# A two-layer recurrent kernel: four chunks' gated products halved by GpSimd for f16 down products, gates turned sooner

## The reference

```python
xn = layernorm(x)
# recurrent part
x_in, res = split(xn @ W_in)                    # 256 channels each
xc = silu(causal_conv4(x_in) + conv_b)
p = xc @ W_x                                    # low rank 16, B 16, C 256
delta = softplus(p[:16] @ W_dt + b_dt)
h = h * delta_t + B_t * x_t                     # per step of the sequence
y = h.sum(states) * C_t
s = (y * silu(res)) @ W_out
# experts: 2 shared and 16 routed, 64 wide
shared = gelu(xn @ shared_up) @ shared_down
gate = top 4 of softmax(xn @ router_w.T), others 0
routed = sum over experts of (gelu(xn @ up) * gate) @ down
x = x + s * silu(shared + routed)
```

## Time and profile before

| what | value |
|---|---|
| median of 3 runs | 686.22 us (683.71 to 689.05) |
| the profiled execution, whole | 683.87 us |
| its span, first to last instruction | 682.1 us |
| TensorE matmul busy | 630.9 us, 93% |
| VectorE busy | 630.7 us, 92% |
| ScalarE busy | 506.7 us, 74% |
| GpSimd busy | 280.0 us, 41% |
| granted TensorE clock, mean | 0.999 of full |
| start of the second layer's body 1 | 291.79 us |

### The profile page before, as it was taken

How to read it: one execution, slowest core, us unless ns; L and a number is a source line. 1 busy time by engine, 2 the same in 40 slices (tenths; PEclk the granted TensorE clock), 3 DMA queues, 4 the chain that set the end, 5 groups by cost and what they waited for, 6 DMA issues and landing times. The chain is left out here.

```text
span 682.1 us, 10868 instructions
## 1 busy us (share of the span) xinstructions
PE 630.9 (93%) x2714; PEld 301.5 (44%) x2714; DVE 630.7 (92%) x1470; ACT 506.7 (74%) x808; POOL 280.0 (41%) x275
## 2 busy tenths in 40 slices
PE   4779999999999997889999999999999999999985
PEld 2334444444444443444444444444444444444442
DVE  4999999999999999989999999999999999999866
ACT  2846666666666665887887888888789788888874
POOL 6557777777676765133122212303303221230220
PEclk9999999999999999999999999999999999999999
DMA  7331000000000000000000000000000000000000
GB/s 174 106 94 31 0 1 0 0 0 0 0 0 0 0 0 0 1 1 0 17 17 0 16 15 0 16 15 0 15 15 15 0 15 15 0 15 15 0 16 31
DMA packets 10739, 11.29 MB, mean 17 GB/s; under 512 B 4800, under 2 KB 6288, under 8 KB 10720
## 3 DMA queue, kind: packets, MB, share of 16 engines
q1 hardware_dynamic: 9744, 10.73, 5.3%
q0 software_dynamic: 112, 0.33, 0.1%
q10 hardware_dynamic: 864, 0.00, 0.1%
HBM read 6.87 MB, written 4.19 MB: 16 GB/s over the span
## 5 line engine op out<-in xcount | busy, mean ns | idle before, releaser
L1177 PE MATMUL bank<-arena,w 128*128 128x512 f16 x640 | 148.6, 379 | 4.0 <-DVE arena L788 4.0
L1177 PE MATMUL bank<-arena,dnT 128*128 128x512 f32 x288 | 138.6, 592 | 0.0
L662 ACT ACTIVATE arena<-bank,xinv 128x512 f32<-128x512 f32 x144 | 94.8, 688 | 37.7 <-PE bank L1177 37.5
L444 POOL TENSOR_TENSOR arena<-arena 128x512 f32<-128x512 f32 x48 | 59.7, 1273 | 135.5 <-ACT arena L599 135.5
L1177 PEld LDWEIGHTS bank<-arena,w 128*128 128x128 f16 x640 | 62.5, 98 | 78.2 <-issue 10.0
L491 ACT ACTIVATE arena<-bank 128x512 f16<-128x512 f32 x96 | 53.9, 607 | 35.6 <-PE bank L1177 35.6
L434 POOL TENSOR_TENSOR arena<-arena 128x512 f32<-128x512 f32 x16 | 16.8, 1051 | 151.6 <-DVE arena L1025 151.6
L1177 PEld LDWEIGHTS bank<-arena,dnT 128*128 128x128 f32 x288 | 53.7, 191 | 35.9 <-issue 21.2
L1177 PE MATMUL bank<-arena,wsqT 128*128 128x512 f32 x128 | 64.5, 608 | 4.7 <-DVE arena L797 4.7
L1034 DVE SCALAR_TENSOR_TENSOR arena<-bank,cws,arena 128x506 f32<-128x506 f32 (+1 forms) x96 | 67.0, 740 | 1.1
L788 DVE SCALAR_TENSOR_TENSOR arena<-bank,arena 128x512 f16<-128x512 f32 x96 | 60.2, 670 | 2.4 <-ACT arena L491 1.2
(11 more groups left out here) (223 smaller groups left out, 1497.7 us busy)
## 6 DMA issues: line engine op xcount, KB each, us to landing
x_all<-in_L_attn_x SPq DMA_DIRECT2D x16, 256.0 KB, 2.6
out<-x_all SPq DMA_DIRECT2D x16, 256.0 KB, 2.0
up_n<-in_L_ffn_routed_up SPq DMA_DIRECT2D x1, 512.0 KB, 4.0
dn_n<-in_L_ffn_routed_down SPq DMA_DIRECT2D x1, 512.0 KB, 5.6
wx<-in_L_attn_W_x SPq DMA_DIRECT2D x1, 288.0 KB, 2.8
k_u<-in_L_ffn_k POOLq DMA_DIRECT2D x1, 256.0 KB, 5.7
w_in<-in_L_attn_W_in SPq DMA_DIRECT2D x1, 256.0 KB, 2.7
k_u<-in_L_ffn_k SPq DMA_DIRECT2D x1, 128.0 KB, 6.6
```

The source lines that it names most:

```text
L444: g.tensor_tensor(prod[:, c, :], act[:, c + 1, :], gate[:, :], ALU.mult).then_inc(sem["b_actp"], 1)
L662: a.activation(act[:, c, :], q_U[(c + 1) % 2][:, :], ACT.Gelu, scale=xinv[:, I_UP:I_UP + 1]).then_inc(sem["b_act"], 1)
L1177: return nc.tensor.matmul(ps, lhsT, rhs, start=start, stop=stop)
```

## The change

GpSimd now has four chunks (GP = 4, chunks 1 to 4) and splits each product into two f16 halves: a product in f32 into `pp` (two buffers), a copy to f16 (`ph`) and the rest as f16 (`pl`). It does this in two pairs per body: chunks 3 and 4 of group m behind the square root for the next group's normalisation, and chunks 1 and 2 of group f behind the spreading of f's gates. VectorE keeps chunks 5 to 8. Down products 1 to 4 become three f16 matmuls each, with weights `dnH` and `dnL`; 0 and 5 to 8 stay f32. To keep halves in range, the down weights are scaled by a power of two, the gates by another, and `ffn_silu` undoes both through its scale; the largest down weight is found by one more Abs pass on ScalarE. The gates are turned behind up product 3 and copied behind Gelu 4 (before: 5 and 8). The up products use three banks in turn, `q_D[0]` and both `q_U`, except in body 0, and down products 5 and 6 move between 2, 3 and 4. The diff, cut to its core:

```diff
@@ build
-    GP = 3
+    GP = 4
     GV = RC - GP
@@ tiles
-        prod = tile(1, [P, RC, N])
+        prod = tile(1, [P, GV, N])
+        pp = tile(1, [P, 2, N])
+        ph = tile(1, [P, GP, N], F16)
+        pl = tile(1, [P, GP, N], F16)
@@ banks
+        q_E = (q_D[0], q_U[0], q_U[1])
+        def up_bank(n, c):
+            return q_U[(c + 1) % 2] if isinstance(n, int) and n == 0 else q_E[c % 3]
@@ GpSimd
+            def gated_halves(m, c):
+                def product(c):
+                    pool.wait_ge(sem["b_act"], UC * m + c + 2)
+                    if not c % 2:
+                        after(pool, sem["b_down"], UC * m if c else UC * (m - 1) + 3)
+                    pool.wait_ge(sem["b_gate"], m + 1)
+                    if c % 2:
+                        pool.wait_ge(sem["b_p"], GP * m + c)
+                    g.tensor_tensor(pp[:, c % 2, :], act[:, c + 1, :], gate[:, :], ALU.mult).then_inc(sem["b_p"], 1)
+                def high(c):
+                    g.tensor_scalar(ph[:, c, :], pp[:, c % 2, :], 1.0, None, ALU.mult).then_inc(sem["b_ph"], 1)
+                def low(c):
...
+                    g.tensor_tensor(pl[:, c, :], pp[:, c % 2, :], ph[:, c, :], ALU.subtract).then_inc(sem["b_actp"], 1)
+                product(c)
+                product(c + 1)
+                high(c)
+                low(c)
+                high(c + 1)
+                low(c + 1)
             def layer1(n):
-                if has(m):
-                    for c in range(GP):
...
-                        g.tensor_tensor(prod[:, c, :], act[:, c + 1, :], gate[:, :], ALU.mult).then_inc(sem["b_actp"], 1)
                 if has(f) and has(f + 1):
                     spread_of_rows(f + 1, "b_")
+                if has(m):
+                    gated_halves(m, 2)
                 if has(f):
                     spread_gates(f)
+                    gated_halves(f, 0)
@@ ScalarE
-                    a.activation(gate[:, :], q_Q[:, :], ACT.Copy).then_inc(sem["b_gate"], 1)
+                    a.activation(gate[:, :], q_Q[:, :], ACT.Copy, scale=down[:, GATE_S:GATE_S + 1]).then_inc(sem["b_gate"], 1)
-                    a.activation(gp[:, :], q_F[:, :], ACT.Silu).then_inc(sem["b_g"], 1)
+                    a.activation(gp[:, :], q_F[:, :], ACT.Silu, scale=down[:, SUM_S:SUM_S + 1]).then_inc(sem["b_g"], 1)
                         if c == 5 and has(f + 1):
                             turned_high(f + 1, 1 - par, q_D[1])
-                    gates_out()
+                        if c == 4:
+                            gates_out()
@@ VectorE
             def down_out(i):
-                v.tensor_copy(dnT[:, i * WB * P:(i + 1) * WB * P], q_W[UB + i][:, 0:WB * P]).then_inc(sem["prep_out"], 1)
+                for c in full:
+                    at_c = max(0, c - GP) * P
+                    last = v.tensor_scalar(dnT[:, at_c:at_c + P], q_W[UB + i][:, c * P - at:(c + 1) * P - at],
+                                           col(down, SHARED_S) if c == 0 else col(wsc, I_DN), None, ALU.mult)
+                if split:
+                    w = slice((split[0] - 1) * P, split[-1] * P)
+                    last = halves(dnH[:, w], dnL[:, w], q_W[UB + i][:, w.start + P - at:w.stop + P - at], col(wsc, I_DN))
+                last.then_inc(sem["prep_out"], 1)
                     gated(GP + 3)
-                    gated(GP + 4)
@@ TensorE
-            DOWN_BEHIND = {1: 5, 3: 6, 6: 7, 7: 8}
+            DOWN_BEHIND = {0: 4, 5: 7, 7: 8}
                 def low_rank():
                     after(pe, sem["b_cr"], IC * m)
+                    if not (isinstance(m, int) and m == 0):
+                        pe.wait_ge(sem["b_act"], UC * m + UC - 2)
                 def expert_in(c):
...
+                    elif c >= 3:
+                        pe.wait_ge(sem["b_act"], UC * f + c - 2)
+                    elif c:
+                        pe.wait_ge(sem["b_conv"], IC * f * (TAPS - 1) + CONV_DONE[c - 1])
                     else:
+                        pe.wait_ge(sem["b_cr"], IC * m + IC)
                 def expert_out(c):
...
+                    if 0 < c <= GP:
+                        mm(q_F[:, :], dnH[:, w], ph[:, c - 1, :], False, False)
+                        mm(q_F[:, :], dnH[:, w], pl[:, c - 1, :], False, False)
+                        last = mm(q_F[:, :], dnL[:, w], ph[:, c - 1, :], False, False)
                     expert_out(2)
+                    expert_out(5)
                     expert_out(3)
-                    expert_out(4)
+                    expert_out(6)
-                    if has(f) and c == 5:
+                    if has(f) and c == 3:
                         gates_turned()
```

More of the change, by code:

```diff
@@ L59, in build @@
     assert G % 2 == 0
-    GP = 3
+    GP = 4
     GV = RC - GP
-    I_IN, I_UP, I_RW, I_WX, I_DT, I_CW, I_CB = range(7)
-    NSC = 7
+    I_IN, I_UP, I_RW, I_WX, I_DT, I_CW, I_CB, I_DN = range(8)
+    NSC = 8
     XC_S, C_FAC, B_FAC, D_FAC = range(4)
+    SHARED_S, SUM_S, GATE_S = range(3)
     x_d = A["L0_attn_x"].rearrange("b t c -> (b t) c").rearrange("(g p j) c -> g p (j c)", p=P, j=J)
@@ L133, in build @@
         fac = sb("fac", [P, 4])
+        down = sb("down", [P, 3])
         cws = sb("cws", [P, IC, TAPS])
-        dnT = sb("dnT", [P, UC * P])
+        dnT = sb("dnT", [P, (UC - GP) * P])
+        dnH = sb("dnH", [P, GP * P], F16)
+        dnL = sb("dnL", [P, GP * P], F16)
         wcH = sb("wcH", [P, IC, DI], F16)
@@ L915, in scales @@
                 v.tensor_scalar(col(fac, B_FAC), col(fac, C_FAC), DS / ZS, None, ALU.mult)
+                v.tensor_scalar(col(down, GATE_S), col(wsc, I_UP), 2.0 ** -3, None, ALU.mult)
+                v.scalar_tensor_tensor(col(down, SHARED_S), col(wsc, I_UP), 2.0 ** -3, col(wsc, I_DN), ALU.mult, ALU.mult)
+                v.scalar_tensor_tensor(col(down, SUM_S), col(inv, I_UP), 2.0 ** 3, col(inv, I_DN), ALU.mult, ALU.mult)
                 v.scalar_tensor_tensor(col(fac, D_FAC), col(fac, C_FAC), 1.0 / ZS, col(inv, I_DT),
@@ L955, in down_out @@
                 dve.wait_ge(sem["prep_turned"], UB + i + 1)
-                v.tensor_copy(dnT[:, i * WB * P:(i + 1) * WB * P], q_W[UB + i][:, 0:WB * P]).then_inc(sem["prep_out"], 1)
+                at = i * WB * P
+                full = [c for c in range(i * WB, (i + 1) * WB) if c == 0 or c > GP]
+                split = [c for c in range(i * WB, (i + 1) * WB) if 0 < c <= GP]
+                for c in full:
[6 more added lines that the diff above has]
+                last.then_inc(sem["prep_out"], 1)
             def turned_low(n, par=0, ps=q_T):
@@ L1045, in gated @@
                     dve.wait_ge(sem["b_gate"], m + 1)
-                    v.tensor_tensor(prod[:, c, :], act[:, c + 1, :], gate[:, :],
+                    v.tensor_tensor(prod[:, c - GP, :], act[:, c + 1, :], gate[:, :],
                                     ALU.mult).then_inc(sem["b_actg"], 1)
```

36 lines of the change are left out of this document (21 added, 15 removed).

## The result

The changed kernel takes 751.03 us (median of 4 runs, 750.44 to 752.71) against 685.76 us before on the same chip: a ratio of 1.095, 95% interval 1.090 to 1.100. It is slower by 65 us. The forecast was 764, with a range from 700 to 800, so direction and range held and the size was 13 us too high. The profiled execution has a span of 748.8 us, 66.7 more than before.

What follows compares the result with a forecast made beforehand. TensorE, working 23.7 of 24.38 us, was taken to set the old period, and VectorE, blocked by GpSimd, the new 29.6. From 683.87: 15 x 5.2 = +78, head +2.9, tail -1.2, Abs +0.2 gave 764, range 700 to 800.

Steps and rivals of the forecast that it cites:

- Part 4: GpSimd's twelve operations per body, 12 us, alternate one for one with VectorE's two-input SBUF operations; period 29.6, 5.2 us more.
- Rival 1: VectorE keeps the port through back-to-back instructions and GpSimd yields: D of 1.5 to 4, times 688 to 726; chance 0.18.
- Rival 3: GpSimd itself bounds, with copies at 1.2 and waits for VectorE: D up by some 2 us, 795; chance 0.08.
- D: Time per body that GpSimd blocks VectorE, added to VectorE's period of 22.88: forecast 6.7 us, bounds 3 to 9.3.
- M: Moment VectorE starts the router maximum: T0 + 3.11 before the change, T0 + 2.80 at the earliest after it.
- Window A: GpSimd's chunks 3 and 4 beside VectorE's normalising and gated products, ahead of `output_weight(1)`: 2.2 us.
- Window B: GpSimd's chunks 1 and 2 beside VectorE's last two scans, two `output` and two `low_xc`: six operations, 4.5 us.
- Prices of one contact: VectorE's loss per GpSimd operation met, scaled from an addition's 0.93: product 1.0, subtraction 0.88, copy 0.37 us.
- the 801 that the rule gave: Time if the shared port lock held for whole instructions: D of 9.2 instead of 6.7, about 801 us.
- T0: Body's start, where TensorE starts the `low_rank` matmuls; claimed to wait for `low_xc`, with 0.06 us for the signal.
- The TensorE part: f16 down products save 0.86 us, three banks remove a 0.67 hole, `output_weight(1)` adds 0.53: TensorE bound 23.38, time 669.
- Head and tail: Head +2.9: weight scaling +1.1, `low_xc` of body 0 +1.8; Abs pass +0.2; tail -1.2, gated product and gate copy off.

Runs made afterwards that it cites:

- experiment 1: Kernel before plus two GpSimd products per body into a scratch tile, beside VectorE's scans: 710.24 us, ratio 1.031.
- experiment 2: Kernel before plus two extra GpSimd products per body, released by the square root to stand beside VectorE's convolution: 685.78 us, ratio 0.999.
- experiment 5: Changed kernel without GpSimd's copies and subtractions, products written directly to f16, high half in the low half's place: 709.57 us, ratio 1.033.
- experiment 8: Kernel before with three up-product banks (up product 2 waiting for `output_weight(1)`) and chunk 4's gated product on GpSimd in f32: 673.13 us, ratio 0.980.
- experiment 9: Changed kernel with GpSimd's high halves written by the copy instruction instead of a multiplication by 1.0: 759.34 us, ratio 1.108.
- experiment 3: Kernel before plus one GpSimd product and two f32 to f16 copies (multiplications by 1.0) beside the scans: 708.04 us, ratio 1.031.
- experiment 4: Kernel before with only the up products in three banks, ordered so up product 2 waits for `output_weight(1)`: 679.58 us, ratio 0.991.
- experiment 6: Changed kernel with the gates turned behind up product 5 and copied behind the last Gelu, as before the change: 761.58 us, ratio 1.109.

## Why the prediction was right, and where its sizes were off

**The mechanism** (Part 4: wide GpSimd operations alternate with VectorE's two-input ones) is shown. Experiments 1 and 2 separate it from GpSimd's load, 5 and 8 from the other parts of the change. Rival 1, in which VectorE keeps the port through back-to-back instructions, falls too: its middle was 708, and four scans issued back to back took 3.46 with a product among them. Rival 3, GpSimd or its copies as the price, was nearer to the copies' length (1.2) and had the consequence wrong: with copies of 1.78 the kernel is at 751, and with short ones it is slower.

**D, per body.** Forecast 6.7, measured 4.9. It can be read in a second way beside the groups: over the 15 periods the mean from the router maximum M to the end of `low_xc` is 24.95 us, and 24.95 - 20.02 = 4.93. The terms:

- Window A: forecast 2.2 from four contacts, measured 2.24 in the body shown from three. The second copy (0.3 in the forecast) cost nothing, and the other three cost 0.30, 0.96 and 0.98 where 0.25, 0.84 and 0.84 stood; the last of them fell on the caps, which the forecast did not count. The window is right; that the sum agrees to 0.04 is luck.
- Window B: forecast 4.5, measured 3.36 in the body shown and less in others (below). This is the step that failed: six contacts were counted and four took place. The term mis-sized below it is the copy, taken at 0.6 from the row with uint8 input, outside its own bound of 1.2 and in truth 1.5 to 1.9. The second copy and subtraction (0.37 + 0.88 in the prediction's prices) came after `low_xc`: 4.5 - 1.25 = 3.25, close to the 3.36. The copy's length explains the one and not the other: with short copies (experiment 9) the second copy meets `low_xc`, and the second subtraction still comes too late, five contacts and 3.71. The other reason is that the contacts hold up GpSimd too, which the window left out: its two products took 3.33 beside the scans and 2.63 alone.
- Prices of one contact: 1.0 for a product (measured 1.03 in experiment 5, 0.8 in experiment 1) and 0.88 for a subtraction (0.89 on `low_xc`, 0.96 and 0.98 in window A) are about right. The 0.37 for a copy agrees (0.37 in experiment 3, if its product costs 0.8 as in experiment 1), but by luck: in proportion to the addition's 0.93 a copy of 0.6 would cost 0.47, and the real one lasts 1.48.

Beside the length of the GpSimd instruction when nothing holds it up, these prices are 0.8 of 1.04 (experiments 1 and 2), 1.03 of 1.24, 0.89 to 0.98 of 1.16, and 0.35 of 0.60 for the short copy of experiment 9 on `low_xc`: all but 0.2 to 0.3 us of it. The slow copy alone stands out, with 0.37 of 1.48.

The Trainium skill ("SBUF — State Buffer", section "SBUF: two separate sides") speaks of an exclusive lock for the whole instruction. That VectorE's two-input work is held up agrees. The length agrees to 0.2 to 0.3 us for the two-input instructions and the short copy, and not at all for the slow copy: 0.37 us for one of 1.70 (experiment 3). The measurement decides, and the 801 that the rule gave is 50 too high, in part for the contacts that did not take place.

**The period.** M came at T0 + 2.80 in ten of fifteen bodies as worked out, and 0.3 to 1.2 later in five, 3.10 on average; in those five `low_rank` ran slowly, 1.33 to 1.91 us instead of 1.03, at half clock (last section). With 24.95 and a gap of 0.31 from the end of `low_xc` to the next T0 (0.06 in the forecast) that makes 28.36. Against 29.58: +0.30, -1.77, +0.25. The 0.31 has two sources: in some bodies T0 follows `w_out`, and in some TensorE is slow. Two small figures of the prediction do not follow from its own sum (D of 4 gives 723 and not 726, D of 2.7 gives 704 and not 700); nothing hangs on them.

**A second pattern of window B.** The five bodies with a late M have no longer periods than the rest (26.66 to 28.97). In three of them, and in the first body, window B has another form. The body that starts at 523.95 shows it:

```profile
545.13 2.43 DVE L1137 TENSOR_TENSOR_SCAN arena<-arena 128x256 f32<-128x256 f32 x4
...
548.66 3.43 DVE L1123 SCALAR_TENSOR_TENSOR arena<-arena,fac 128x512 f16<-128x512 f32 x2
...
547.92 3.62 POOL L458 TENSOR_TENSOR arena<-arena 128x512 f32<-128x512 f32 x2 [5.32 <-PE bank L1226]
```

TensorE was slow at up product 0, the gates came late, and GpSimd met only `low_xc`: 2.02 instead of 3.36. What TensorE loses there is given back by fewer contacts. The prediction held one pattern for all bodies.

**The TensorE part.** The f16 down products at 0.215 each came true; so did the new wait for `output_weight(1)`. Its 0.53 can't be seen in the changed kernel, where window A makes it 2.45. In experiment 5, with window A free, TensorE would reach up product 0 at 510.14 and issues it at 510.67: 0.53 from issue to issue, 0.37 of it idle by the modelled ends. (The prediction counts four f16 products ahead of it; the queue has three, 1 to 3, and the 0.22 is right for three.) TensorE's own bound (23.38, time 669) was never reached, so no run tests it; experiment 8, with f32 products, runs at the bound of that form, 23.7 forecast and 23.73 measured.

**What T0 waits for.** The prediction took `low_xc`. Experiments 4 and 5 show that `output` through `w_out` binds about 0.6 earlier where `low_xc` is undisturbed. In the changed kernel `low_xc` carries its own 0.89, so its path is the later one again, and this omission cost the forecast little. It cost both expectations of 4 and 5.

**Head and tail.** Forecast +2.9, +0.2 and -1.2; measured 296.04 - 291.79 = +4.25 for the head, and 748.80 - 721.45 = 27.35 against 24.68 for the tail, +2.67. In the head the down weights' scaling costs 1.6 (forecast 1.1), with its last piece, for which T0 waits, behind `low_xc`; the contact with `low_xc` of body 0 costs 0.4 (forecast 1.8). The other 2.3 us are there before the scaling starts, and the prediction has 0.2 for them, the Abs pass. They are mostly a difference from one execution to another: experiment 4, without that pass, has 1.8 of them at the end of the first layer, and experiment 5, with it, 0.3. The tail's sign was wrong: GpSimd works on the last group until 731.8, the scans start 1.2 us later after T0, and `w_out` takes 3.10 us there instead of 1.98, at a granted clock of 0.62.

The account: 15 x 3.99 = 59.8, head 4.25, tail 2.67: the 66.7 us of the span.

## What to carry to other kernels

Before work is moved to GpSimd, list which of VectorE's instructions read two SBUF tiles (here also `tensor_scalar`s from SBUF to SBUF), and put GpSimd's work beside the others; the same two products cost nothing in one place and 24 us in another. Count what meets rather than busy time: a GpSimd instruction that meets such an instruction of VectorE costs about its own undisturbed length less 0.2 to 0.3 us, and the slow copies far less, so making them shorter can let more of them meet. Let both engines' delays move the windows when the contacts are counted. And try the parts of a bundled change apart: two of these gained 12.5 us, and with the rest on top the kernel is 78 slower than with these two.

## What the runs showed of the hardware that was not expected

**A copy's form.** GpSimd's f32 to f16 pass over 512 columns took 1.48 at least and 1.78 on average as a multiplication by 1.0, and about 0.61 undisturbed (0.83 on average) as a copy instruction. The slow form blocked VectorE by 0.37 us all the same (experiment 3).

**TensorE's clock can fall behind pauses.** Before, the granted clock between the first and the last T0 was 1.00 of full. In the changed kernel's view by stretches (columns: stretch, its length, busy time by engine with counts, granted clock, DMA share, GB/s):

```profile
510.00:513.00 3.00, 2.97 (x16) 1.66 (x17) 2.79 (x19) 2.70 (x4) 1.04 (x1) 1.00 0.00 0
...
523.95:525.80 1.85, 1.85 (x6) 0.75 (x5) 1.62 (x6) 0.00 (x0) 1.77 (x2) 0.50 0.00 0
...
539.86:543.20 3.34, 3.34 (x8) 1.18 (x9) 3.13 (x19) 1.93 (x2) 1.04 (x1) 0.51 0.02 6
```

Behind the pause of 2.45 us at 510.03 the clock stays full. Behind the 2.24 us at `w_out` it falls, during its four matmuls, to half (1.2 GHz instead of 2.4), and four `low_rank` matmuls take 1.91 instead of 1.03. In the next body up product 0 starts at 539.86, again behind a pause of 2.45, and there it is down to 0.51. The mean between the first and the last T0 is 0.96. In experiment 5, with pauses of 0.37 and 1.83 per body, the granted clock was 1.00 from 319.63 to 625.53. Which pauses bring a drop and which do not these runs do not tell. So a wait can cost TensorE more than its own length. In the changed kernel little of that reached the end: the gap of 0.31 holds at most 0.25 of it per body and the late M another 0.30, 8 us in all, and the three late bodies with fewer contacts give back 1.34 each. In experiment 6 it sets T0.
